# A new order of all engine queues in a six-layer local-attention kernel: each block of score or value matmuls stands alone on TensorE

## The reference

```
for i in range(DEPTH):                      # 6
    x = attn_layer(shift_tokens(x), Wqkv[i], q_scale[i], k_scale[i], Wo[i]) + x
    x = ffn_layer(shift_tokens(x), ln_g[i], ln_b[i], W1[i], b1[i], W2[i], b2[i]) + x
```

## Time and profile before

| | |
|---|---|
| three runs | 3290.15, 3290.96, 6130.29 us; median 3290.96 |
| the profiled execution's own time | 3280.19 us |
| its span, from the first to the last instruction | 3278.2 us |
| PE busy (matmul) | 3104.7 us, 95% |
| PE weight load, DVE, ACT, POOL busy | 2401.1, 2710.0, 2761.7, 2562.8 us |
| granted TensorE clock | 0.993 on the mean |
| instructions | 154299, of which 65674 MATMUL and 66148 LDWEIGHTS records |

### The profile page before, as it was taken

One profiled execution on the slowest core, in us unless ns is written; L12 is line 12 of the kernel. 1 busy time (PEld: TensorE's weight loads), 2 busy tenths in 40 slices (PEclk: granted clock), 3 DMA queues, 4 the chain that ended last, 5 costly groups with the idle time before them and its releaser, 6 DMA issues.

```text
span 3278.2 us, 154299 instructions
## 1 busy us (share of the span) xinstructions
PE 3104.7 (95%) x65674; PEld 2401.1 (73%) x66148; DVE 2710.0 (83%) x4034; ACT 2761.7 (84%) x4817; POOL 2562.8 (78%) x2557
## 2 busy tenths in 40 slices
PE   8998799999999999999999999999989999999998
PEld 6886477777777777777776777777767777777776
DVE  6886788888887788888887888888878888888884
ACT  5665688989988889998888899988889999888886
POOL 3433888888888788888888888887878888787883
PEclk9999899999999999999999999999999999999999
DMA  1000322332223232223322223332222332322231
GB/s 46 29 3 28 82 74 66 85 78 71 72 70 88 59 77 74 74 67 87 85 56 75 72 68 81 85 75 63 71 72 70 85 75 71 81 75 64 62 75 52
DMA packets 140218, 224.67 MB, mean 69 GB/s; under 512 B 29456, under 2 KB 41360, under 8 KB 139152
## 3 DMA queue, kind: packets, MB, share of 16 engines
q1 hardware_dynamic: 139536, 214.78, 25.6%
HBM read 21.72 MB, written 4.19 MB: 8 GB/s over the span
## 4 chain that ended last, share of the span: by engine, by line
PE 89%; issue 6%; POOL 3%; DVE 1%; ACT 1%; POOLq 0%; DVEq 0%; ACTq 0%
PE bank L1021 11%; PE bank L954 11%; PE bank L1037 10%; PE bank L906 9%; PE bank L1367 8%; PE bank L980 8%; PE bank L907 7%; PE bank L999 5%; PE bank L905 4%; PE bank L1380 4%; POOL rotbuf L1298 2%; PE bank L364 2%; PE bank L344 2%; PE bank L329 2%; PE bank L1352 1%
## 5 line engine op out<-in xcount | busy, mean ns | idle before, releaser
L1284 POOL TENSOR_TENSOR rotbuf<-mbuf 128x512 f32<-128x512 f32 x768 | 969.4, 1274 | 402.6 <-PE bank L954 380.3
L1298 POOL TENSOR_TENSOR rotbuf<-rotbuf,rs 128x512 f32<-128x512 f32 x768 | 784.6, 1042 | 7.5
L1173 DVE TENSOR_TENSOR mbuf<-bank,table 128x512 f32<-128x512 f32 x768 | 519.8, 677 | 137.8 <-ACT sq L1063 124.4
L1174 DVE TENSOR_TENSOR mbuf<-bank,table 128x512 f32<-128x512 f32 x768 | 521.8, 679 | 0.0
L1063 ACT ACTIVATE sq<-bank 128x512 f32<-128x512 f32 x768 | 458.7, 597 | 51.4 <-PE bank L907 27.7
L906 PE MATMUL bank<-weights,inputs 128*128 128x512 bf16 x1152 | 441.0, 383 | 46.1 <-issue 13.3
L1155 DVE TENSOR_REDUCE ss<-sq 128x16 f32<-128x1024 f32 x384 | 463.7, 1208 | 0.0
L1021 PEld LDWEIGHTS bank<-probs_t,vbuf 64*64 64x64 f32 x24576 | 380.5, 135 | 91.9 <-issue 60.1
L954 PE MATMUL bank<-ident,rotbuf 128*128 128x128 f32 x3072 | 427.3, 276 | 15.9 <-issue 6.4
L907 PE MATMUL bank<-weights,inputs 128*128 128x512 bf16 x1152 | 440.7, 383 | 0.0
L1021 PE MATMUL bank<-probs_t,vbuf 64*64 64x32 f32 x24576 | 404.7, 220 | 17.9 <-issue 17.6
(11 more groups left out here) (119 smaller groups left out, 5773.6 us busy)
## 6 DMA issues: line engine op xcount, KB each, us to landing
vbuf<-v_stage SPq DMA_DIRECT2D x1152, 128.0 KB
vbuf<-v_stage SPq DMA_DIRECT2D x576, 64.0 KB
stage<-in_wqkv SPq DMA_DIRECT2D x36, 256.0 KB, 2.9
weights<-in_wo SPq DMA_DIRECT2D x6, 512.0 KB, 4.0
out_t<-weights SPq DMA_DIRECT2D x1, 2048.0 KB, 6.3
weights<-out_t SPq DMA_DIRECT2D x1, 2048.0 KB, 11.3
out_t<-weights SPq DMA_DIRECT2D x16, 128.0 KB, 2.1
wffn<-in_w SPq DMA_DIRECT2D x6, 341.0 KB, 3.1
```

Source lines behind the costliest of these rows:

```text
L1173: e.tensor_tensor(b.m1[:, u % 2, :].rearrange("p (h s d) -> p h s d", h=8, s=2), pj, cos, ALU.mult)
L1174: e.tensor_tensor(b.m2[:, u % 2, :].rearrange("p (h s d) -> p h s d", h=8, s=2), pj[:, :, ::-1, :], sin, ALU.mult).then_inc(s.pj_free, 1)
L1284: e.tensor_tensor(b.rot[:, u, :], b.m1[:, u % 2, :], b.m2[:, u % 2, :], ALU.add).then_inc(s.rotated, 1)
L1298: e.tensor_tensor(v, v, r, ALU.mult).then_inc(s.scaled, 1)
```

## The change

The four lists and the ring get a new order; no step is added, removed or altered, and SP's list stays. The diff, cut to the ring and the start of two lists (the lists of ACT, DVE and POOL change in the same way, and their start is also rotated: some steps that closed a slot now open the next one with an offset one lower):

```diff
@@ -43,10 +43,10 @@
 WORK_RING = (
-    ("t", 6, 1), ("t", 7, 1), ("pj", 0, 3), ("v", 1, 2), ("mu", 0, -1), ("pj", 1, 3), ("dn", 0, -2),
...
+    ("t", 6, 1), ("pj", 7, 2), ("up", 2, -2), ("pj", 0, 3), ("t", 7, 1), ("v", 1, 2), ("mu", 0, -1),
...
@@ -1597,144 +1597,144 @@
 def pe_deep_slot(e, s, b, at):
 
     pe_transpose(e, s, b, at, 1, 6)
-    pe_transpose(e, s, b, at, 1, 7)
+    pe_project_in(e, s, b, at, 2, 7)
+    pe_ff_up(e, s, b, at, -2, 2)
+    pe_values_of(e, s, b, at, 0, 1)
...
-    pe_values_of(e, s, b, at, 1, 1)
...
 def act_deep_slot(e, s, b, at):
 
+    act_mask(e, s, b, at, 0, 1)
+    act_exp_of(e, s, b, at, 0, 0)
...
```

More of the change, by code:

```diff
@@ L1613, in pe_deep_slot @@
     pe_transpose(e, s, b, at, 2, 1)
-    pe_values_in(e, s, b, at, 2, 2)
     pe_project_in(e, s, b, at, 3, 2)
     pe_scores_of(e, s, b, at, 1, 2)
+    pe_values_in(e, s, b, at, 2, 2)
+    pe_values_in(e, s, b, at, 2, 3)
     pe_scores_of(e, s, b, at, 1, 3)
-    pe_values_in(e, s, b, at, 2, 3)
     pe_transpose(e, s, b, at, 2, 2)
@@ L1627, in pe_deep_slot @@
     pe_project_in(e, s, b, at, 3, 5)
+    pe_transpose(e, s, b, at, 2, 5)
+    pe_transpose_probs_of(e, s, b, at, 1, 0)
     pe_ff_up(e, s, b, at, -1, 0)
-    pe_transpose_probs_of(e, s, b, at, 1, 1)
-    pe_transpose(e, s, b, at, 2, 5)
     pe_scores_of(e, s, b, at, 2, 0)
@@ L1633, in pe_deep_slot @@
     pe_project_in(e, s, b, at, 3, 6)
-    pe_ff_up(e, s, b, at, -1, 2)
-    pe_project_in(e, s, b, at, 3, 7)
+    pe_transpose_probs_of(e, s, b, at, 1, 1)
     pe_values_of(e, s, b, at, 1, 0)
-    pe_values_of(e, s, b, at, 1, 1)
 def act_deep_slot(e, s, b, at):
+    act_mask(e, s, b, at, 0, 1)
+    act_exp_of(e, s, b, at, 0, 0)
+    act_copy_t(e, s, b, at, 1, 0)
+    act_square(e, s, b, at, 2, 2)
     act_copy_t(e, s, b, at, 1, 1)
+    act_copy_out(e, s, b, at, -1, 1)
     act_copy_v(e, s, b, at, 1, 2)
-    act_square(e, s, b, at, 2, 2)
-    act_copy_out(e, s, b, at, -1, 1)
     act_copy_v(e, s, b, at, 1, 3)
@@ L1650, in act_deep_slot @@
     act_square(e, s, b, at, 2, 4)
+    act_mask(e, s, b, at, 1, 0)
     act_input_of(e, s, b, at, 3)
@@ L1658, in act_deep_slot @@
     act_square(e, s, b, at, 2, 5)
+    act_copy_t(e, s, b, at, 1, 5)
+    act_copy_pt_of(e, s, b, at, 0, 0)
+    act_ff_shift(e, s, b, at, -1)
     act_ff_gelu(e, s, b, at, -2, 0)
-    act_copy_t(e, s, b, at, 1, 5)
     act_ff_gelu(e, s, b, at, -2, 1)
+    act_square(e, s, b, at, 2, 6)
     act_copy_pt_of(e, s, b, at, 0, 1)
-    act_square(e, s, b, at, 2, 6)
-    act_ff_shift(e, s, b, at, -1)
+    act_copy_t(e, s, b, at, 1, 6)
     act_square(e, s, b, at, 2, 7)
     act_ff_gelu(e, s, b, at, -2, 2)
-    act_copy_t(e, s, b, at, 1, 6)
-    act_copy_t(e, s, b, at, 1, 7)
     act_square(e, s, b, at, 3, 0)
     act_copy_pt_of(e, s, b, at, 0, 2)
+    act_copy_out(e, s, b, at, 0, 0)
+    act_copy_t(e, s, b, at, 1, 7)
     act_seed(e, s, b, at, 2)
-    act_copy_out(e, s, b, at, 0, 0)
+    act_copy_pt_of(e, s, b, at, 0, 3)
+    act_copy_v(e, s, b, at, 2, 1)
     act_ff_square(e, s, b, at, -1)
-    act_copy_pt_of(e, s, b, at, 0, 3)
     act_square(e, s, b, at, 3, 1)
-    act_copy_v(e, s, b, at, 2, 1)
     act_ff_seed(e, s, b, at, -1)
-    act_mask(e, s, b, at, 1, 1)
-    act_exp_of(e, s, b, at, 1, 0)
-    act_copy_t(e, s, b, at, 2, 0)
 def dve_deep_slot(e, s, b, at):
-    dve_sum_squares(e, s, b, at, 2, 2)
-    dve_rope(e, s, b, at, 2, 6)
-    dve_ff_gate(e, s, b, at, -2, 2)
-    dve_rope(e, s, b, at, 2, 7)
-    dve_sum_squares(e, s, b, at, 2, 3)
     dve_clamp(e, s, b, at, 2)
     dve_rope(e, s, b, at, 3, 0)
+    dve_max_of(e, s, b, at, 1, 0)
     dve_ff_centre(e, s, b, at, -1)
-    dve_max_of(e, s, b, at, 1, 0)
     dve_shift(e, s, b, at, 1, 0)
@@ L1707, in dve_deep_slot @@
     dve_sum_squares(e, s, b, at, 3, 1)
+    dve_rope(e, s, b, at, 3, 5)
     dve_sum_of(e, s, b, at, 1, 1)
-    dve_rope(e, s, b, at, 3, 5)
+    dve_sum_squares(e, s, b, at, 3, 2)
     dve_ff_gate(e, s, b, at, -1, 0)
     dve_ff_gate(e, s, b, at, -1, 1)
+    dve_rope(e, s, b, at, 3, 6)
+    dve_rope(e, s, b, at, 3, 7)
+    dve_ff_gate(e, s, b, at, -1, 2)
+    dve_sum_squares(e, s, b, at, 3, 3)
 def pool_deep_slot(e, s, b, at):
+    pool_scale(e, s, b, at, 1, 4)
+    pool_scale(e, s, b, at, 1, 5)
+    pool_rotate(e, s, b, at, 2, 3)
     pool_input_of(e, s, b, at, 3)
+    pool_scale(e, s, b, at, 1, 6)
+    pool_rotate(e, s, b, at, 2, 4)
     pool_rotate(e, s, b, at, 2, 5)
+    pool_normalise_of(e, s, b, at, 0, 1)
     pool_scale(e, s, b, at, 1, 7)
-    pool_normalise_of(e, s, b, at, 0, 1)
     pool_rotate(e, s, b, at, 2, 6)
```

23 lines of the change are left out of this document (8 added, 15 removed), and 6 rows, old and new, of the table WORK_RING.

## The result

| | before | after |
|---|---|---|
| median of the runs side by side | 3290.96 us (3290.15 to 3296.14) | 3261.94 us (3261.48 to 3262.19, 4 runs) |
| ratio of after to before, 95% interval | | 0.9923 (0.9906 to 0.9940) |
| profiled execution, its span | 3280.19, 3278.2 us | 3262.19, 3260.4 us |
| good slot, L1037 to L1037 | 29.26 us | 29.91 us |
| the 91 slots | 2759.4 us | 2745.3 us |

(The execution of 6130.29 us among the runs of before is left out.) The change makes the kernel 0.8% faster; 0.4% slower was forecast. The time lies in the range, on the other side of no change. The last row but one is 2759.4 - 91 x 29.26 and 2745.3 - 91 x 29.91. The last row is worked out from the trace's LDWEIGHTS records of L980 and L1021, from start to start, so its microseconds are somewhat more than the idle time of the earlier trace rows.

The account below looks back on a forecast made before the run. PE was taken as the bound, its period the sum of its steps. Slot growth +85 us, outside the window +4, pauses -69 and scattered waits -7 gave 3293; 10.8 us carried over made 3303 us, range 3255 to 3345.

Parts of the forecast that it names:

- blocks: value alone against half a pair: In PE's value blocks: one alone takes 1.05 us, against 1.00 us as half a pair.
- entries, 3 more a slot: On PE, the last normal matmul step before a small-matmul block takes 0.09 us longer.
- exits, 3 more a slot, and what the score pair hid: On PE, going from a small-matmul block back to normal matmuls loses 0.09 us on average.
- new data waits: PE at L954 after `down` and at the last `up`: 0.15 us a slot, from 0 to 0.35.
- pauses and scattered waits: PE's pauses inside small blocks fall from 76 us to 7; scattered waits fall by 7 us.
- outside the 91 slots: The five instances outside the measured window add 4 us.
- carried over from profile to median: The median shown lay 10.8 us above the profiled execution; this was added to 3293 us.
- 2.95 us of cover: Between small blocks on PE: work must last 2.95 us until the next instructions come, read from one score pair.
- Rival A: Block borders on PE are free and only the pauses go: 3208 us, chance 0.06.
- Rival B: Pauses stay in value block 3 and score blocks 2 and 3, with borders on top: 3380 us, chance 0.08.
- the rule that the Trainium skill states on the fetch: Instruction stream: refilled in blocks of 256, fetch hidden, so pauses have another cause and a new order need not remove them.
- Rival C: A new wait each slot through ACT's queue or the last `up`, from 0.6 us a slot: 3344 us, chance 0.11.

Follow-up runs that it names:

- after again: The changed kernel, unedited, run once more on the same chip as a rerun of the kernel before: median 3258.28 us, ratio 0.9935.
- before again: The kernel before, unedited, run once more beside itself: 3273.42 to 3284.16 us, profiled execution 3282.86 us.
- the kernel with the short chain: The changed kernel without L1468, a DVE step that refines the norm: 3251.98 us, good slot 29.80 us.
- all splits in the order before: The kernel before with the score pair and both value pairs split on TensorE's list alone, other queues unchanged: 3344.16 us, ratio 1.0213.
- the seed first: The changed kernel with one pair of ACT's list swapped, the norm's seed ahead of a projection's square: 3399.22 us, ratio 1.0364.
- four runs with one gap: The changed kernel with TensorE's already covered waits left out and no dummy instructions: 3249.79 us (3245.96 to 3251.72).

## Why the prediction was wrong

The profiled execution was forecast at 3293 and took 3262.19, 31 us less. By the terms of the sum, each as 91 slots where it is one of a slot:

| term | forecast | measured | difference |
|---|---|---|---|
| blocks: value alone against half a pair, 4 a slot | 0.20 us | 0.27 | +6 us |
| entries, 3 more a slot | 0.27 | 0.28 | +1 |
| exits, 3 more a slot, and what the score pair hid | 0.31 | 0.07 | -22 |
| a data wait of the order before that is gone | 0 | -0.08 | -7 |
| new data waits | 0.15 | 0.11 | -4 |
| the slots' growth | 0.93, 85 us | 0.65, 59 us | -26 |
| pauses and scattered waits | -76 us | -73 | +3 |
| outside the 91 slots | +4 us | -4 | -8 |
| carried over from profile to median | +10.8 us | -0.3 | -11 |

(96.7 - 23.5 = 73 in the pauses' row. Outside, the first deep L1037 starts at 394.6 us instead of 399.2; after again and before again show the same 4 us, 395.8 and 399.8. Why is not tested.)

**What failed: the price of an exit.** The forecast took "0.09 on exit on average, since two of the new exits lead to bf16 projections, where none shows after the score pair". It saw the right row and averaged it away. The exit depends on what follows the block. Read from the timelines of after and of the kernel with the short chain, less the missing L905 records, it is 0.10 us to L1367, 0.11 to L1380, 0.06 to L954 and L999, 0.01 to a projection. The sum over a slot is 0.34 us before and 0.41 after. In the order before, four of the five exits were the dear ones (0.10 and 0.06 after the single score blocks, 0.06 and 0.11 after the value pairs, 0.02 after the score pair). The change has eight exits, and three of them lead to projections. The forecast priced its new exits at 0.31 us, by their count; they measured 0.07. That alone moves the sum from +13 to -9 us, and the direction with it.

A second misreading stands beside it. The forecast read 0.14 us of exit at the transposes behind a value pair. Only 0.06 of it is an exit. The other 0.08 are a data wait, which leaves no row on PE. The kernel before, L905's weight load among it:

```profile
1406.84 1.09 PE L954 MATMUL bank<-ident,rotbuf 128*128 128x128 f32 x8
1407.11 0.68 DVE L1174 TENSOR_TENSOR mbuf<-bank,table 128x512 f32<-128x512 f32 x1
1407.84 0.10 PEld L905 LDWEIGHTS bank<-weights,inputs 128*128 128x128 bf16 x1
```

The last transpose starts at 1407.66 and would let the load go out at once. But L1174 is done at 1407.79, and projection 0 follows projection 7 in the bank that L1174 frees (`WORK_RING`). In 86 of the 96 places the load starts 0.05 us after the end of L1174. In the new ring `t` 6 stands there instead, and the wait is gone. With all splits in the order before it is the same wait that grows to 1.0 us. By its own readings, 0.14 among them, a sum of all eight exits one by one would have come to 0.18 us more a slot instead of 0.31, and the whole to about +1 us: the right step, but not yet the sign.

**What was right.** The mechanism: the pauses are the instruction stream running dry, single blocks hardly show it, and some 7 us of 76 would be left; 12.0 us are left by the gaps, nearly all in slots 17 to 24, 39 to 46, 60 to 68 and 81 to 87, the old beat. For the reason why a single block hardly pauses the forecast had one row, and its 2.95 us of cover is not tested by itself. The place of the new data wait, L954 behind `down` for L1470, and its size within 0.04 us. The value block alone at 1.07, inside 1.00 to 1.07. Rival A had the right sign, but its mechanism did not happen: blocks, entries and exits cost 0.62 us a slot, they are not free. Rival B, the pauses stay, is excluded by all runs, and with it the outcome of the rule that the Trainium skill states on the fetch. Rival C needed 0.6 us and got 0.11; where one list moved alone, such a wait did come (0.77 us of idle with all splits in the order before, 1.5 with the seed first).

**The second miss, the carry-over.** The median shown stood 10.8 us above the profiled execution, and the forecast took that as a constant, from two runs. It did not carry over: after's profiled execution is 0.3 us above its median, and the timed runs of before again lie on both sides of its profiled one. What the 10.8 us were stays open. On the four chips of the experiments the kernel before ran at 3268.93 to 3286.75 us, so all three runs beside the change (3290.15 to 3296.14) lie above every later one, and after ran 3.7 us slower there than after again. That points to a difference between chips, not to the spread alone; nor do few pauses always go with a small spread (5.8 us in four runs with one gap, 8.9 with ACT's seed first).

Two smaller points. The forecast counted 0.2 us of refill for each pause; some cost more, which is in the last section. And it read the pauses as a matter of dense blocks alone. They needed dense blocks and a bad place in the packet, else the beat of 21 slots would not be there, and 85 of the same 96.7 us could be had by other means than the order.

## What to carry to other kernels

Price a border by its two neighbours, each read from a row of its own, and never by the number of borders; and look at the weight loads in that row first, since a data wait may be hidden in it. When an engine pauses with no releaser, list the lengths of equal slots in order and lay the ends of the pauses beside the packets of the instruction queue. A beat, and a fixed distance to the packets, point to the instruction stream, and then leaving out waits that are already covered, or moving the start by a few instructions, may do what a new order does, without its cost (here 65 to 78 us against 19 to 29). In a kernel of hand-written queues do not move one queue alone, since the step behind the one that you made earlier may stand ahead of the consumer in a third engine's queue.

## What the runs showed that was not expected

**A pause can cost the clock.** A stretch of the kernel before, in PE's timeline:

```profile
1119.58 1.14 PE L980 MATMUL bank<-kbuf,qbuf 64*32 64x64 f32 x93
1122.66 0.57 PE L980 MATMUL bank<-kbuf,qbuf 64*32 64x64 f32 x35 [1.95 <-issue]
1123.56 0.63 PE L906 MATMUL bank<-weights,inputs 128*128 128x512 bf16 x1 [0.33 <-issue]
1123.99 0.63 PE L907 MATMUL bank<-weights,inputs 128*128 128x512 bf16 x1
1124.42 1.91 PE L954 MATMUL bank<-ident,rotbuf 128*128 128x128 f32 x8
1126.12 0.62 PE L905 MATMUL bank<-weights,inputs 128*128 128x512 bf16 x1
1126.55 0.41 PE L906 MATMUL bank<-weights,inputs 128*128 128x512 bf16 x1
```

and the busy time of all engines in it, with the granted clock in the third column from the end:

```profile
1123.30:1126.60 3.30, 3.04 (x12) 2.22 (x12) 2.45 (x2) 1.43 (x3) 0.97 (x1) 0.50 0.46 104
```

After 1.95 us without work the granted clock is 0.50, the lower of its two levels (1.2 of 2.4 GHz), for some 3 us: eight transposes take 1.70 us to the next start instead of 0.87, a projection 0.43 instead of 0.22. The pause costs about half of that stretch, 1.5 us, on top of its idle time. Counted by projections of 0.5 us and more, the kernel before has four such stretches in the deep layers, before again seven, after none, after again one. A pause of the stream is not needed for it: in after the granted clock is 0.57 from 2839 to 2843 us, where PE had waited 2.73 us for ACT at the start of a layer.

**Covered waits are not free.** Eleven wait instructions a slot, none of which ever waited for anything, cost the kernel before 65 us, while its good slot stays at 29.26 us with or without them. They fill packets and bring the drift of 12 places; how these two parts divide is open: at places of the bad kind the gaps fell to 24.5 us, so the shorter stream helps there too, and why is not shown.

**A data wait can hide between two rows.** Like the wait for L1174 in the section before, the wait for `mu`'s bank, 0.11 us a slot or 10 us of the kernel, shows only at the weight load (26.9 us in 88), with no row on PE. Neither number is its price: taking a step out of the chain gave it.
